# Summing more rows of a bucket beside the tile loop: 96, 128, 160, 192 by visit in place of 96

## The reference

```python
x = layernorm(x + L0(x))      # degree-normalised sum of neighbours' rows
x = layernorm(x + L1(x))      # gated messages, below
# L1: gate = silu(edge_attr @ W1.T + b1) @ W2.T + b2 + <emb[type src], emb[type dst] @ adaptW.T>
#     msg  = gate * h[dst] * (cutoff(distance) * mult[dst])
#     agg  = segment_sum(msg, src) / segment_sum(mult[dst], src)
#     out  = layernorm(h + agg) * gamma + beta
```

## Time and profile before

| | |
|---|---|
| median of three runs | 3067.45 us (3059.66 to 3067.46) |
| span of the profiled execution | 3050.1 us |
| its own time | the profile gives the span alone; the median is 17.35 us above it |
| instructions | 73627 |
| stretch of the gathers (tiles 0 to 100) | 240.6 to 2711 us |
| tiles still in work behind the last gather | 2711 to 2819 us |
| last stage | 2819 to 3050 us |

### The profile page before, as it was taken

One profiled execution on the slowest core, in us unless ns is written; L12 is line 12 of the kernel. 1 busy time (PEld: TensorE's weight loads), 2 busy tenths in 40 slices (PEclk: granted clock), 3 DMA queues, 4 the chain that ended last, 5 costly groups with the idle time before them and its releaser, 6 DMA issues. The chain is left out here.

```text
span 3050.1 us, 73627 instructions
## 1 busy us (share of the span) xinstructions
PE 2251.7 (74%) x25909; PEld 1913.8 (63%) x25909; DVE 2404.4 (79%) x5424; ACT 1399.4 (46%) x2929; POOL 2117.9 (69%) x1852
## 2 busy tenths in 40 slices
PE   6970477678787787777787878787878788876674
PEld 5860366566666675666676767676666666665664
DVE  9994577778787787877788788888888888875886
ACT  7982244444444454444444444444444444444122
POOL 7506777877777777777777777777777777750241
PEclk9665688888888898888888889888888988888887
DMA  8405233344434444333454444554545444452984
GB/s 314 152 7 158 61 111 112 104 119 121 117 112 119 122 125 114 113 112 114 123 155 145 144 145 145 146 147 142 158 132 163 150 155 145 143 146 81 419 327 174
DMA packets 174620, 441.51 MB, mean 145 GB/s; under 512 B 92296, under 2 KB 92296, under 8 KB 154440
## 3 DMA queue, kind: packets, MB, share of 16 engines
q1 hardware_dynamic: 103388, 236.05, 23.4%
q0 software_dynamic: 67888, 194.98, 21.9%
q10 hardware_dynamic: 3004, 5.90, 0.6%
HBM read 292.51 MB, written 144.27 MB: 143 GB/s over the span
## 5 line engine op out<-in xcount | busy, mean ns | idle before, releaser
L722 POOL DMA_INDIRECT slot<-table,gidx x1616 | 1827.3, 1131 | 617.3 <-issue 606.8
L821 PEld LDWEIGHTS route<-parts,oh_r 128*128 128x128 bf16 x11312 | 758.0, 99 | 88.9 <-issue 64.1
L821 PE MATMUL route<-parts,oh_r 128*128 128x148 bf16 x11312 | 806.4, 231 | 3.4 <-DVE parts L1224 3.0
L1089 DVE TENSOR_SCALAR oh_r<-iota_r,spot 128x896 bf16<-128x896 f16 x1616 | 613.5, 450 | 75.4 <-PE route L821 75.3
L894 ACT ACTIVATE routed<-route 128x444 bf16<-128x444 f32 (+1 forms) x1010 | 508.8, 514 | 250.2 <-PE route L821 234.8
L856 PE MATMUL pwin<-slot,oh_d 128*128 128x144 bf16 x1616 | 175.6, 284 | 424.0 <-DMA slot<-table,gidx 392.1
L856 PEld LDWEIGHTS pwin<-slot,oh_d 128*128 128x128 bf16 x1616 | 153.8, 156 | 448.6 <-issue 291.6
L777 PEld LDWEIGHTS pwin<-win,oh_t 128*128 128x128 bf16 x4848 | 258.8, 115 | 180.8 <-issue 96.1
L747 PE MATMUL phid<-attr,w 80*96 80x512 f32 x404 | 285.8, 798 | 48.6 <-issue 47.7
L777 PE MATMUL pwin<-win,oh_t 128*128 128x80 bf16 (+1 forms) x4848 | 272.6, 225 | 54.4 <-ACT ssum L904 49.4
L1195 DVE TENSOR_TENSOR prod<-slot,got 128x256 f32<-128x256 f32 x202 | 84.7, 419 | 243.1 <-ACT parts L955 243.0
(11 more groups left out here) (228 smaller groups left out, 3211.3 us busy)
## 6 DMA issues: line engine op xcount, KB each, us to landing
rows<-slots SPq DMA_DIRECT2D x51, 1295.0 KB, 10.1
oh_t<-dst_row SPq DMA_DIRECT2D x101, 512.0 KB
erows<-slots SPq DMA_DIRECT2D x51, 777.0 KB
attr<-in_edge_attr SPq DMA_DIRECT2D x101, 320.0 KB
slots<-zeros SPq DMA_DIRECT2D x53, 518.0 KB
slot<-table,gidx POOLq DMA_INDIRECT x1616
table<-tab SPq DMA_DIRECT2D x3, 676.0 KB, 6.0
weight_t<-weights SPq DMA_DIRECT2D x101, 8.0 KB
```

The source lines that it names most:

```text
L722: e.indirect_dma_start(out=slot[:, s, g, :], out_offset=None, in_=table0, in_offset=bass.IndirectOffsetOnAxis(ap=gidx[:, s, g:g + 1], axis ...
L821: mm = e.matmul(route[:, (NPH * m + phase) % 2, RC * (j - a):RC * (j - a + 1)], oh_r[:, c, slot_of, :], parts[:, s % 2, c, :], start=(c == ...
L1089: oh = e.tensor_scalar(oh_r[:, c], iota_r[:, :, :], spot[:, s % 2, c:c + 1], None, ALU.is_equal)
```

## The change

The number of rows summed early grows with the visit: 96 for visits 0 to 15, 128 for 16 to 29, 160 for 30 to 41 and 192 for 42 to 50. In units of 28 x rows / 128 columns these are 21, 28, 35 and 42. The last stage loads and sums the rest, 35, 28, 21 or 14 columns. The order of the visits changes too: buckets 36 to 50 first (visits 0 to 14), then 0 to 35. `eoh`, `emine` and `erows` are 42 columns wide, `rows`, `onehot` and `count` stay 35 wide and are used in part. The test ahead of the loop asks for each bucket's own number.

Each early step that depends on the number of rows is made once for each range of `VISITS`, six in all: (0,1), (1,15), (15,16), (16,30), (30,42), (42,51). `over_tiles` takes a first and a last tile for a step. It makes a hardware loop of consecutive turns of six iterations only where the same steps are active in all iterations of at least two turns; every other turn is written out.

```diff
-EARLY = 96
-ECOLS = EARLY * R // P
-COLS = (CAP - EARLY) * R // P
+TURNED = 15
+GROUPS = ((0, 96), (16, 128), (30, 160), (42, 192))
+def bucket_of(v):
+    return v + NB - TURNED if v < TURNED else v - TURNED
+EARLY = {bucket_of(v): max(rows for first, rows in GROUPS if first <= v) for v in range(NB)}
+ECOLS = max(EARLY.values()) * R // P
+COLS = (CAP - min(EARLY.values())) * R // P
...
-    if late:
-        until, again = (min(late) - n % slots) // slots, -(-(max(late) - n % slots) // slots)
-        looped(a, until, False)
-        unrolled(range(until * slots + n % slots, again * slots + n % slots))
-        looped(again, b, True)
-    else:
-        looped(a, b, False)
+    a = first // slots
+    while a < n // slots:
+        same, b = active(a * slots + rest), a
+        while b < n // slots and all(active(b * slots + rest + k) == same for k in range(slots)):
+            b += 1
+        if b > a + 1:
+            looped(a, b)
+        else:
+            b = a + 1
+            unrolled(range(a * slots + rest, b * slots + rest))
+        a = b
...
-                        for c in range(ECOLS):
-                            mm = e.matmul(esums, eoh[:, :, c], erows[:, c, 0:3 * MW], start=(c == 0),
-                                          stop=(c == ECOLS - 1))
+                            cols = rows * R // P
+                            for c in range(cols):
+                                mm = e.matmul(esums, eoh[:, :, c], erows[:, c, 0:3 * MW], start=(c == 0),
+                                              stop=(c == cols - 1))
...
-                        for a in range(0, ECOLS, G):
-                            b = min(a + G, ECOLS)
-                            oh = e.tensor_tensor(eoh[:, :, a:b], number[:, :, 0:b - a], bc_mid(emine[:, a:b], P),
-                                                 ALU.is_equal)
+                            for c in range(0, cols, G):
+                                d = min(c + G, cols)
+                                oh = e.tensor_tensor(eoh[:, :, c:d], number[:, :, 0:d - c], bc_mid(emine[:, c:d], P),
+                                                     ALU.is_equal)
...
-                                e.dma_start(rows[:, b % RS].rearrange("p a c -> p (a c)"),
-                                            slots[R * (CAP * b + EARLY):R * CAP * (b + 1), :].rearrange(
+                                e.dma_start(rows[:, b % RS, 0:cols(b)].rearrange("p a c -> p (a c)"),
+                                            slots[R * (CAP * b + EARLY[b]):R * CAP * (b + 1), :].rearrange(
...
-                                e.tensor_tensor(onehot[:, b % OS], count[:, :, :], bc_mid(mine[:, b % OS], P),
-                                                ALU.is_equal).then_inc(ohs, 1)
+                                e.tensor_tensor(onehot[:, b % OS, :, 0:cols(b)], count[:, :, 0:cols(b)],
+                                                bc_mid(mine[:, b % OS, 0:cols(b)], P), ALU.is_equal
+                                                ).then_inc(ohs, 1)
...
-                            for c in range(COLS):
+                            for c in range(cols(b)):
```

More of the change, by code:

```diff
@@ L83, in over_tiles, with active, looped @@
 def over_tiles(e, n, slots, *steps):
[L87 to L90, removed]
+    steps = [(step, lag, *(within or (0, n))) for step, lag, *within in steps]
+    rest = n % slots
+    first = slots + rest + (slots if max(lag for _, lag, *_ in steps) > rest else 0)
+    assert all(lag <= first - slots for _, lag, *_ in steps)
+    def active(t):
+        return tuple(begin <= t - lag < end for _, lag, begin, end in steps)
     def unrolled(times):
         for t in times:
[L94 to L95 removed]
+            for (step, lag, *_), on in zip(steps, active(t)):
+                if on:
                     step(*divmod(t - lag, slots))
[L98 removed]
+    def looped(a, b):
         with e.Fori(a, b) as turn:
             for k in range(slots):
[L101 to L103 removed]
+                for (step, lag, *_), on in zip(steps, active(a * slots + rest + k)):
+                    if on:
+                        ahead, s = divmod(rest + k - lag, slots)
                         step(turn + ahead if ahead else turn, s)
[L105 removed]
     unrolled(range(first))
[L107 to L114 removed]
+    a = first // slots
[9 more added lines that the diff above has]
+        a = b
+    unrolled(range(n, n + max(lag for _, lag, *_ in steps)))
 def since(i, s, n):
@@ L641, in visit, with in_visits, begun @@
                 return U * i + s - EARLY_FROM
-            def visited(i, s):
+            def in_visits(of):
+                return [(of(a, rows), EARLY_FROM + a, EARLY_FROM + b) for a, b, rows in VISITS]
+            def begun(i, s):
                 v = visit(i, s)
-                return (v + 1) % NB if isinstance(v, int) else v + 1
-            def visits(i, s):
-                return 0 <= visit(i, s) < NB if isinstance(i, int) else True
+                return not isinstance(v, int) or v > 0
             def pair_of(i, s):
@@ new lines, in early_rows, with step @@
+                    def early_rows(a, rows):
+                        def step(i, s):
+                            v = visit(i, s)
+                            if not begun(i, s):
+                                for par in range(2):
+                                    e.wait_ge(scattered[par], 16 * ((EARLY_FROM - 3 - par) // 2 + 1))
+                            else:
+                                e.wait_ge(esummed, v)
+                            e.dma_start(erows[:, 0:rows * R // P, :].rearrange("p a c -> p (a c)"),
+                                        slots[bass.ds((v + (bucket_of(a) - a)) * (R * CAP), R * rows), :].rearrange(
+                                            "(p a) c -> p (a c)", p=P)).then_inc(erows_in, 16)
+                        return step
@@ L1581, in _ @@
                                     e.wait_ge(ohs, b - OS + 1)
-                                e.activation(mine[:, b % OS], rows[:, b % RS, :, RC - 1], ACT.Copy
+                                e.activation(mine[:, b % OS, 0:cols(b)], rows[:, b % RS, 0:cols(b), RC - 1], ACT.Copy
                                              ).then_inc(keyed, 1)
```

127 lines of the change are left out of this document (61 added, 66 removed).

## The result

The changed kernel takes **3121.1 us** (median of four runs, 3105.14 to 3129.06) where the kernel before takes 3067.45 beside it (four runs, 3059.66 to 3079.56): a ratio of 1.0168, 95% interval 1.0133 to 1.0202, so 1.3% to 2.0% slower. The forecast was 3096, within 3052 to 3114: the sign was right, the loss 25 us too small, and the measured time lies above the range. The profiled execution has a span of 3103.3 us, 53.2 more than before.

A forecast was written before the change was run, and what follows sets the result against it. GpSimd's gather queue was taken to set the tile loop's pace, VectorE to bound the last stage. -22 + 10 + 5 + 36 = +29 us took the span from 3050.1 to 3079; with 17.35 around it 3096, range 3052 to 3114.

The forecast's parts named there:

- held gathers: GpSimd gathers beside written-out VectorE turns last until VectorE's chain ends: 4 to 8 us, every second tile from 64.
- Turns written out, +36: Tile loop, gathers of tiles 64 to 99: written-out VectorE code beside them makes gathers longer, taken as 36 us more.
- The bound of 47: Tile loop: price of written-out turns for 36 tiles at 1.3 us each, 47 us, if nothing else changes.
- Columns added to the tile loop, +10: Tile loop: added one-hots and matmuls lie under TensorE's wait for gathers; gathers slowed by VectorE cost 10 us.
- rival 3: Tile loop, 42-column visits: the early sum becomes the bound, some 50 us, 3145; chance 0.05.
- Behind the last gather, +5: Visits 49 and 50, with no gathers to cover added one-hots, matmuls and larger loads: 5 us more, bounds 0 and 12.
- The last stage, -22: Last stage: fewer columns shorten VectorE's one-hots, so the stage takes 22 us less, bounds -12 and -34.
- the stall behind SP's stores: Last stage: one-hots' wait behind SP's output stores grows from 2.95 us to 5 to 8, twice; taken as +3 net.
- the prediction's formula: Last-stage one-hots: 0.553 ns an element and 0.077 us fixed; 0.2 us was added for a broken row.
- The 17.35 us around the span: Whole kernel: time outside the profiled span, 17.35 us, added to the predicted span of 3079 to give 3096.
- Rivals 1 and 2: Tile loop from 64: held gathers don't come back, about 3060, chance 0.20; or half come back, 3078, chance 0.17.
- rival 1: Tile loop: held gathers don't come back; -7, with the stage's bounds -19 to +8, about 3060; chance 0.20.

The follow-up runs named there:

- e8: Changed kernel with TensorE's early sum put ahead of the first 56 routing matmuls; 1.0089 of the kernel before.
- e12: Changed kernel with one added VectorE wait, for its own bucket one-hots, ahead of the first eight routing one-hots; 1.0087 of the kernel before.
- e9: e8 with one added VectorE wait, for its own bucket one-hots, ahead of the first eight routing one-hots; 0.9897 of the kernel before.
- e11: Kernel before with only the added VectorE wait for its bucket one-hots ahead of the first eight routing one-hots; 0.9940.
- e1: Kernel before, without growth, with VectorE's iterations from 53 on written out and other engines looped; 1.0220.
- e3: Changed kernel with ranges moved to 19, 31 and 43 and single turns looped, so TensorE and VectorE loop through 53 to 100; 1.0229 of the kernel before.
- e10: Kernel before, without growth, with TensorE's early sum put ahead of the first half of the routing matmuls; 0.9970.
- b1: e3 with the next tile's index load issued ahead of the early rows' load; 1.0246 of the kernel before.
- b3: e7 with the next tile's index load issued ahead of the early rows' load; 0.9980 of the kernel before.
- e7: e3 with TensorE's early sum put ahead of the first 56 routing matmuls; 0.9975 of the kernel before.
- e2: Kernel before, without growth, with SP's, TensorE's and ScalarE's iterations from 53 on written out and VectorE looped; 0.9959.
- b4: e7 with growth to 160 rows only, in place of 192; 0.9966 of the kernel before.

## Why the prediction was wrong

Four kernels make a square of the two causes:

| ratio to the kernel before | ring as changed | ring shortened |
|---|---|---|
| gathers held | 1.0211 | 1.0089 (e8) |
| gathers not held | 1.0087 (e12) | 0.9897 (e9) |

Each mended alone gives 0.012, both together 0.031. But the wait also takes away held gathers that the kernel before had too, worth 0.006 (e11), most of them ahead of tile 64. So of the changed kernel's own held gathers only about 0.006 is won while the ring stands, and 0.013 with the ring short; these runs come from different sets, so neither is good to better than 0.004. Tiles 64 to 99 alone, in us against the kernel before (891), say it more plainly: held gathers alone +51 (e1) and +53 (e8), the ring alone +76 (e3, with three held gathers) and +68 (e12), both +81 and +84. Where both stand, the ring costs nearly all and the held gathers lie under it, presumably since a GpSimd that is held is not waiting for an index load (argued, not shown).

So the right sign was in part luck. The forecast's loss rested on held gathers; these came, but without them the kernel would have been as slow (e3, 1.0229), by a cause that the forecast had at 10 us.

By the prediction's own steps:

- *Turns written out, +36.* The mechanism held: e1 makes it alone, e9 takes it away by a pause. The size was cut too far. 36 tiles held 18 gathers, and the extra busy time is 54.3 us. The bound of 47 was there; the 11 us taken off for an overlap with what looped tiles lose to one-hots was the wrong way, since e1's 36 tiles cost 26.2 us each, 1.4 more than looped ones and not 1.0. The earlier trace rows had shown the late kind at 4.06; the mean here is 5.0.
- *Columns added to the tile loop, +10.* The step that failed: "Both lie under TensorE's wait for gathers, 2.5 us a tile". A mean wait of one engine was taken as cover for a chain through ScalarE, VectorE, TensorE and SP's queue, whose end starts it again. The wait covered nothing: in e3's tiles from 83 on TensorE waits 2.5 us a tile for gathers, and a tile takes 29.1 us. It was rival 3, given 0.05 with 4 us a tile for seven visits and half for twelve, some 50 us; e3 shows 4.5 to 5 and 3.9. Rival 3 was put aside since "sums, keys and one-hots each have most of an iteration": each has, but all together have one round of 24.8 us, of which e10 shows no more than 3 as slack. The trace had what is needed: the load's issue, the copy, the one-hots and the sum give the ring in the kernel before, 5.3 + 0.6 + 2.0 + 14.9 + 1.5.
- *The index load* stood in no sum. The diff adds bytes to the DMA ahead of it on SP's queue. It made waits of up to 8.32 us; b1 and b3, without these waits, are no faster than e3 and e7: they cost nothing of their own.
- *Behind the last gather, +5:* measured +15, and +10 in the second profiled execution. Early sums are left there too, with the ring as long as before them; how the 15 us divide was not measured by itself.
- *The last stage, -22:* measured -31.8. Narrow one-hots came at 2.147, 1.679 and 1.243 us (taken: 2.26, 1.76, 1.27), 28 us in place of 25, and the stall behind SP's stores did not grow (at most 3.08 us ahead of a one-hot, 2.95 before), while idle time fell by 3. The Trainium skill ("Vector Engine (DVE) Microarchitecture Reference", section 5.1) says that two-source ops on 16-bit data pair their elements over the whole stream, rows of odd length included. By that the prediction's formula would hold at each width, 2.06, 1.56 and 1.07; the rows here lie 0.09 to 0.17 us above it.
- *The 17.35 us around the span* was no such thing. The changed kernel's profiled execution took 3105.14 us with a span of 3103.3, 1.8 around it, and the other runs have 1.75 to 2.97. So the kernel before's median run had a span some 15 us longer than its profiled one. This didn't move the forecast, since the median of the changed kernel is as far above its profiled run (53.65 us between the medians, 53.2 between the spans).

Rivals 1 and 2, held gathers that stay away or come back by half, were wrong: each even tile from 64 to 100 has one. A slip in rival 1 changes nothing: with the stage's bounds of -34 and -12 it reaches from -19 to +3, not to +8. The Trainium skill ("Runtime: NRT & Kernel Launch", "Instruction fetch mechanics") names taken branches as a reason to prefer full unrolling. Here SP, TensorE and ScalarE written out together gave 0.9959 (e2), VectorE written out 1.0220 (e1): it holds for the three together, and not for VectorE beside GpSimd's gathers.

What stays open: why single gathers were held in e3's tiles 94 to 98 and in e7 and b4, where the loop is intact, and why e2 and e10 are faster. Two buffers for `erows`, which would open the ring outright, were not tried; whether they would fit in SBUF beside `eoh` no run shows.

## What to carry to other kernels

Before a step is made larger, follow its buffer around: from the release to the load, through each engine to the next release. If the ring with what you add is longer than the pace, every us beyond it counts, on whatever engine and however idle that one is on average. A ring as long as the pace may still hold slack; move one step and see. The cheapest mend here was to move the step that releases the buffer forward in its engine's order. When two causes may cover each other, take both away before judging either; and a pause in VectorE's run of one-hots can be worth more than the time it takes, where GpSimd sets the pace: it gave the unchanged kernel 0.6%.

## What the runs showed of the hardware

A GpSimd gather of 0.94 us lasts 4 to 5.7 us when VectorE's one-hots (1.21, 0.57 and 2.98 us) run without a pause beside it; with one semaphore wait between them the longest of e9's 576 is 3.43, and in tile 10 of e11 2.27. That it is register work which makes the pauses in a loop was only argued. SP's, TensorE's and ScalarE's code, written out, made the kernel 0.2% to 0.6% faster. One-hots of `eoh` took 1.224 us 16 columns wide, 0.957 at 12, 0.817 at 10, 0.854 at 5 and 0.776 at 3:

```profile
L1197 DVE TENSOR_TENSOR eoh<-number,emine 128x1536 bf16<-128x1536 bf16 x14 | 13.4, 957 | 0.0
L1197 DVE TENSOR_TENSOR eoh<-number,emine 128x384 bf16<-128x384 bf16 x12 | 9.3, 776 | 0.0
L1197 DVE TENSOR_TENSOR eoh<-number,emine 128x1280 bf16<-128x1280 bf16 x6 | 4.9, 817 | 0.0
L1197 DVE TENSOR_TENSOR eoh<-number,emine 128x640 bf16<-128x640 bf16 x3 | 2.6, 854 | 0.0
```

The instruction with rows of 5 costs more than the one with rows of 10, and one of 3 columns is nearly as dear as one of 10.
